# Two graph layers and routed experts on one core: further blocks in pairs, ring slots marked in fours

## What is computed

```python
h = relu(rgcn_conv(layernorm(x), W1, Wroot1, b1))     # both layers: the same edges
x = x + rgcn_conv(h, W2, Wroot2, b2)
x = x + experts(layernorm(x))                         # 2 of 8 experts for each node
# rgcn_conv:
xs = x[src]
seg = dst * R + etype
sums = segment_sum(xs, seg, N * R); cnt = segment_sum(ones, seg, N * R)
mean = (sums / maximum(cnt, 1)[:, None]).reshape(N, R, -1)
return x @ Wroot + b + einsum('nrd,rde->ne', mean, W)
```

## Time and profile before

| | us |
|---|---|
| median of three runs | 2933.71 |
| lowest, highest | 2932.59, 2935.83 |
| span of the profiled execution | 3487.9 |
| PE, VectorE, ScalarE busy in it | 2472.0, 1780.8, 1225.2 |
| GpSimd busy in it | 1862.5 |
| gathers L509 | 1584 of 964 ns |

### The profile page before, as it was taken

How to read it: one execution, slowest core, us unless ns; L and a number is a source line. 1 busy time by engine, 2 the same in 40 slices (tenths; PEclk the granted TensorE clock), 3 DMA queues, 4 the chain that set the end, 5 groups by cost and what they waited for, 6 DMA issues and landing times.

```text
span 3487.9 us, 82172 instructions
## 1 busy us (share of the span) xinstructions
PE 2472.0 (71%) x19212; PEld 1832.7 (53%) x19213; DVE 1780.8 (51%) x4984; ACT 1225.2 (35%) x2344; POOL 1862.5 (53%) x1980
## 2 busy tenths in 40 slices
PE   1346787678687786346776587687877428999999
PEld 0113565356365564114564365465656327888887
DVE  7324455345355454124454354354545338787777
ACT  5202343134243342012343143152432126555554
POOL 1666566655655554666556656655563543333333
PEclk9557999589799898557998798798997559999999
DMA  6223323233332232223333333333335234322222
GB/s 216 80 83 112 88 87 91 85 87 89 87 88 87 86 89 64 86 84 97 98 104 97 94 100 99 94 105 95 101 100 163 102 115 132 96 73 71 71 70 59
DMA packets 165489, 333.24 MB, mean 96 GB/s; under 512 B 36078, under 2 KB 102346, under 8 KB 165288
## 3 DMA queue, kind: packets, MB, share of 16 engines
q0 software_dynamic: 91632, 247.48, 24.1%
q1 hardware_dynamic: 39912, 41.03, 4.0%
q10 hardware_dynamic: 33872, 43.92, 3.9%
HBM read 285.39 MB, written 49.07 MB: 96 GB/s over the span
## 4 chain that ended last, share of the span: by engine, by line
PE 44%; issue 22%; DVE 10%; another core or an unknown queue 9%; DVEq 7%; SPq 2%; ACT 2%; DMA 1%; ACTq 0%; POOLq 0%; POOL 0%
PE more_banks L1408 13%; PE sum_banks L1384 9%; PE sum_banks L1385 7%; PE more_banks L1535 4%; PE sum_banks L1535 3%; PE more_banks L1400 3%; PE sum_banks L1545 3%; DVEq L1044 3%; DVEq L1041 2%; DVE sels L1044 2%; DVEq L1027 1%; DVE stage L1079 1%; DVE sels L1036 1%; PE sum_banks L1426 1%
## 5 line engine op out<-in xcount | busy, mean ns | idle before, releaser
L509 POOL DMA_INDIRECT ring<-table,tabs x1584 | 1526.9, 964 | 1046.4 <-SPq L399 670.0
L1384 PE MATMUL sum_banks<-ring,sels 128*128 x2348 | 726.6, 311 | 630.1 <-issue 420.1
L1408 PE MATMUL more_banks<-weights,stage 128*128 128x256 f16 x5292 | 919.1, 290 | 22.0 <-issue 21.4
L1385 PE MATMUL sum_banks<-ring,sels 128*128 x2348 | 732.2, 313 | 41.5 <-issue 38.7
L1384 PEld LDWEIGHTS sum_banks<-ring,sels 128*128 128x128 f16 (+1 forms) x2348 | 242.4, 103 | 928.2 <-issue 896.9
L683 ACT ACTIVATE stage<-sum_banks,inv 128x256 f16<-128x256 f32 x784 | 328.1, 473 | 789.5 <-issue 384.9
L1408 PEld LDWEIGHTS more_banks<-weights,stage 128*128 128x128 f16 x5292 | 531.1, 104 | 135.3 <-issue 37.1
L1036 DVE SCALAR_TENSOR_TENSOR sels<-lane,win_off,tabs 128x256 f16<-128x256 f16 x792 | 349.4, 482 | 422.1 <-remote 181.9
L654 ACT ACTIVATE stage<-more_banks 128x1024 f16<-128x1024 f16 x392 | 402.0, 1026 | 419.1 <-remote 405.6
L1044 DVE TENSOR_SCALAR sels<-lane,win_off,tabs 128x128 f16 x780 | 260.6, 334 | 495.8 <-issue 339.6
L1079 DVE SCALAR_TENSOR_TENSOR stage<-sum_banks,inv,stage 128x256 f16<-128x256 f32 x784 | 347.0, 479 | 57.2 <-issue 40.2
(11 more groups left out here) (319 smaller groups left out, 2407.5 us busy)
## 6 DMA issues: line engine op xcount, KB each, us to landing
ring<-table,tabs POOLq DMA_INDIRECT x1584
weights<-L_ffn_W ACTq DMA_DIRECT2D x96, 178.5 KB
stage<-L_ffn_W ACTq DMA_DIRECT2D x16, 1024.0 KB, 5.0
edge_work<-lot_in SPq DMA_DIRECT2D x54, 260.0 KB
table<-edge_work ACTq DMA_DIRECT2D x49, 128.0 KB
lot_in<-sels SPq DMA_DIRECT2D x8, 260.0 KB
weights<-L_gnn_W SPq DMA_DIRECT2D x2, 1024.0 KB, 8.3
weights<-L_gnn_W ACTq DMA_DIRECT2D x2, 1024.0 KB
```

What stands on the lines that cost most here:

```text
L509: pool.indirect_dma_start(ring_rows[:, b % RING, 0:2 * D], None, tables[layer], bass.IndirectOffsetOnAxis(row_tab[:, b:b + 1], 0)).then_in ...
L1384: pe.matmul(to[:, 0:D + 1], hot, ring_row[:, ds(at + D, D + 1)], start=first, stop=last, skip_group_check=True)
L1385: return pe.matmul(to[:, 0:D], hot, ring_row[:, ds(at, D)], start=False, stop=last, skip_group_check=True)
L1408: return [pe.matmul(ps_out[par], rows[:, xp * KD + k, :], w16[:, wp, k, r * D:(r + 1) * D], start=part == PART_ORDER[0] and n == 0, stop=p ...
```

## The change

Further blocks are taken two at a time. VectorE's loop makes two selections in one operation of 128 x 256, in the next of eight places of `sel_more`, and PE's loop adds two blocks and counts two steps at once. A window with an odd number of further blocks takes one block beyond its end; its selection is all zeros, since no edge of it belongs to the window. Both loops wait for the rows of both blocks. SyncE works in groups of four slots: it waits until four gathers have landed on one semaphore, or until all four slots are done with, and adds four. GpSimd waits for slots at every fourth gather. The setup computes the step counts for the padded numbers: two operations on rows of 392, and six on rows of 784 ahead of `turn_row`'s last use; `free_meta` has one number a group.

```diff
...
@@ -388,30 +396,30 @@
                 store_first(c)
 
             for layer in range(2):
-                regs = [sp.alloc_register(f"sp_free{layer}_{s}") for s in range(RING)]
-
-                def landed(turn, s):
-                    sp.wait_ge(gathered[s], turn * 16 + 16 * (USES[s] * layer + 1))
-                    sp.sem_inc(rows_ready[layer], 1)
-
-                def freed(s):
-                    sp.wait_ge(steps_done[layer], sp.snap(regs[s], donate=True) & MASK)
-                    sp.sem_inc(slots_free[layer], 1)
-                for s in range(AHEAD):
-                    landed(0, s)
+                regs = [sp.alloc_register(f"sp_free{layer}_{g}") for g in range(RING_GROUPS)]
+
+                def landed(turn, g):
+                    sp.wait_ge(gathered[g], turn * (16 * GROUP) + 16 * GROUP * (USES[g] * layer + 1))
+                    sp.sem_inc(rows_ready[layer], GROUP)
+
+                def freed(g):
+                    sp.wait_ge(steps_done[layer], sp.snap(regs[g], donate=True) & MASK)
+                    sp.sem_inc(slots_free[layer], GROUP)
+                for g in range(AHEAD):
+                    landed(0, g)
                 if layer == 0:
                     sp.wait_ge(tabs_set, 3 * COUNT + 3)
                 with sp.Fori(0, TURNS) as u:
-                    sp.load(regs, free_meta[0:1, ds(u * RING, RING)])
-                    for s in range(RING):
-                        freed(s)
-                        landed(u if s < AHEAD else u + 1, (s + AHEAD) % RING)
-                sp.load(regs, free_meta[0:1, TURNS * RING:(TURNS + 1) * RING])
-                for n in range(TURNS * RING, GATHERS - AHEAD):
-                    if n < TURNS * RING + OVER:
-                        freed(n % RING)
-                    landed((n + AHEAD) // RING, (n + AHEAD) % RING)
-                sp.sem_inc(rows_ready[layer], 1)
+                    sp.load(regs, free_meta[0:1, ds(u * RING_GROUPS, RING_GROUPS)])
+                    for g in range(RING_GROUPS):
+                        freed(g)
+                        landed(u if g < AHEAD else u + 1, (g + AHEAD) % RING_GROUPS)
+                sp.load(regs, free_meta[0:1, TURNS * RING_GROUPS:(TURNS + 1) * RING_GROUPS])
+                for n in range(TURNS * RING_GROUPS, GROUPS_ALL - AHEAD):
+                    if n < TURNS * RING_GROUPS + OVER:
+                        freed(n % RING_GROUPS)
+                    landed((n + AHEAD) // RING_GROUPS, (n + AHEAD) % RING_GROUPS)
+                sp.sem_inc(rows_ready[layer], GROUP)
                 for r in regs:
                     sp.free_register(r)
 
...
@@ -504,10 +512,10 @@
                 if layer == 1:
                     pool.wait_ge(table2_out, 16 * TILES)
                 for b in range(GATHERS):
-                    if b >= RING:
-                        pool.wait_ge(slots_free[layer], b - RING + 1)
+                    if b >= RING and b % GROUP == 0:
+                        pool.wait_ge(slots_free[layer], b - RING + GROUP)
                     pool.indirect_dma_start(ring_rows[:, b % RING, 0:2 * D], None, tables[layer],
-                                            bass.IndirectOffsetOnAxis(row_tab[:, b:b + 1], 0)).then_inc(gathered[b % RING], 16)
+                                            bass.IndirectOffsetOnAxis(row_tab[:, b:b + 1], 0)).then_inc(gathered[b % RING // GROUP], 16)
                 pool.drain()
 
             pool.wait_ge(sums_done[1], WPT * 14)
...
@@ -954,12 +962,15 @@
                 v.scalar_tensor_tensor(w_flat16[:, 1, :], w32, gnn_scale[:, layer:layer + 1], w_flat16[:, 0, :], ALU.mult, ALU.subtract).then_inc(w_split, 1)
             v.wait_ge(spans_ps, 2)
             lo, span, more, upto, one = (span_rows[0:1, k, :] for k in range(5))
+            padded = span_rows[0:1, 5, :].bitcast(i32)
             v.memset(one, 1.0)
             v.tensor_copy(lo, bank[4][0:1, 0:WINDOWS])
             link(v.tensor_copy(span, bank[5][0:1, 0:WINDOWS]))
             link(v.tensor_tensor(span, span, lo, ALU.subtract))
             link(v.tensor_scalar(more, span, -2.0, 0.0, ALU.add, ALU.max))
-            link(v.tensor_tensor_scan(upto, one, more, 0.0, ALU.mult, ALU.add))
+            link(v.tensor_scalar(padded, more, PAIR - 1.0, None, ALU.add))
+            link(v.tensor_scalar(padded, padded, (1 << 22) - PAIR, None, ALU.bitwise_and))
+            link(v.tensor_tensor_scan(upto, one, padded, 0.0, ALU.mult, ALU.add))
             v.memset(meta[0:1, WINDOWS:, 0], 2)
             v.memset(meta[0:1, WINDOWS:, 1], 0)
             for r in range(COUNT):
...
@@ -991,7 +1002,14 @@
             link(v.tensor_tensor(turn_row, last_row[:, 2:BLOCKS + 2], last_row[:, 1:BLOCKS + 1], ALU.subtract))
             link(v.scalar_tensor_tensor(left_row, left_row, 1.0, first_row, ALU.min, ALU.max))
             link(v.scalar_tensor_tensor(left_row, turn_row, 2.0, left_row, ALU.mult, ALU.add))
+            v.memset(kept_row[:, 0:1], 0.0)
             link(v.tensor_scalar(turn_row, turn_row, 1.0, None, ALU.min))
+            link(v.tensor_scalar(stay_row, turn_row, -1.0, 1.0, ALU.mult, ALU.add))
+            link(v.tensor_tensor_scan(kept_row[:, 1:BLOCKS + 1], stay_row, one_row, 0.0, ALU.mult, ALU.add))
+            link(v.scalar_tensor_tensor(first_row, kept_row[:, 0:BLOCKS], -1.0, first_row, ALU.mult, ALU.subtract))
+            link(v.tensor_scalar(pad_row, first_row, 2.0, 0.0, ALU.add, ALU.min))
+            link(v.tensor_scalar(pad_row, pad_row, PAIR - 1, None, ALU.bitwise_and))
+            link(v.tensor_tensor(left_row, left_row, pad_row, ALU.add))
             link(v.scalar_tensor_tensor(turn_row, left_row, -2.0, turn_row, ALU.add, ALU.mult))
             link(v.tensor_tensor_scan(free_src[:, 0:BLOCKS], one_row, turn_row, 0.0, ALU.add, ALU.add))
 
...
@@ -1036,13 +1054,18 @@
                 return v.scalar_tensor_tensor(sel[:, slot, h], lane16[:].unsqueeze(1).to_broadcast([P, 2, P]), win_off[:, ds(w, 1)],
                                               key_tab[:, ds((need - 2).with_bounds(min_val=0, max_val=GATHERS - 1), 2)].unsqueeze(2).to_broadcast([P, 2, P]), ALU.add, ALU.is_equal)
 
+            since = v.alloc_register("dve_since")
+
             def more_blocks(layer, need, end, w):
                 with v.If(end > need):
-                    with v.Fori(need & MASK, end) as i:
-                        v.wait_ge(rows_ready[layer], i + 1)
-                        block = i.with_bounds(min_val=0, max_val=GATHERS - 1)
-                        v.tensor_scalar(flat(sel_more[:, ds(block & (RING - 1), 1), :]), lane16[:], win_off[:, ds(w, 1)], key_tab[:, ds(block, 1)],
-                                        ALU.add, ALU.is_equal).then_inc(more_ready[layer], 1)
+                    with v.Fori(need & MASK, end, PAIR) as i:
+                        turn_no = v.snap(since, min_val=1, max_val=MASK)
+                        v.wait_ge(rows_ready[layer], i + PAIR)
+                        spot = ((turn_no & (SPOTS - 1)) * PAIR).with_bounds(min_val=0, max_val=RING - PAIR)
+                        v.scalar_tensor_tensor(sel_more[:, ds(spot, PAIR), :], lane16[:].unsqueeze(1).to_broadcast([P, PAIR, P]), win_off[:, ds(w, 1)],
+                                               key_tab[:, ds(i.with_bounds(min_val=0, max_val=GATHERS - 1), PAIR)].unsqueeze(2).to_broadcast([P, PAIR, P]),
+                                               ALU.add, ALU.is_equal).then_inc(more_ready[layer], 1)
+                        v.reg_add(since, since, 1)
 
             for layer in range(2):
                 def sums_out(t, par):
...
@@ -1388,11 +1413,15 @@
 
                 def more_sums(to, block, end):
                     with pe.If(end > block):
-                        with pe.Fori(block, end) as i:
+                        with pe.Fori(block, end, PAIR) as i:
+                            turn_no = pe.snap(since, min_val=1, max_val=MASK)
                             pe.wait_ge(more_ready[layer], since)
-                            slot = i & (RING - 1)
-                            at = (slot * PITCH).with_bounds(min_val=0, max_val=(RING - 1) * PITCH)
-                            add_rows(to, flat(sel_more[:, ds(slot, 1), :]), at, False, True).then_inc(steps_done[layer], 1)
+                            spot = (turn_no & (SPOTS - 1)) * PAIR
+                            for b in range(PAIR):
+                                hot = flat(sel_more[:, ds((spot + b).with_bounds(min_val=0, max_val=RING - 1), 1), :])
+                                at = ((i + b & (RING - 1)) * PITCH).with_bounds(min_val=0, max_val=(RING - 1) * PITCH)
+                                ins = add_rows(to, hot, at, False, True)
+                            ins.then_inc(steps_done[layer], PAIR)
                             pe.reg_add(since, since, 1)
 
                 def turn(c, slot):
```

(10 more changed lines are left out.)

30 lines of the change are left out of this document (18 added, 12 removed).

## The result

The changed kernel takes **3116.81 us** (median of four runs, 3116.47 to 3119.7) against 2933.72 us for the kernel before in the same comparison: ratio 1.0625, 95% interval 1.061 to 1.064. It is slower by 183 us. The prediction said 3065 us, slower, with a range of 2945 to 3150: the sign and the range held, the size of the loss was given as 131 us, which is 52 us too little.

The account below looks back on a forecast made before the run. Gathers (1.25 us each) bind heavy windows, the PE, VectorE and ScalarE path light ones. Layers 120 us, ends 5 and setup 6 make 131 us: 2933.7 + 131 = 3065 us, range 2945 to 3150.

Parts of the forecast that it names:

- The mechanism: PE's loop: register rows grow nearly as fast as turns fall, so windows with one further block cost 1.50 us against 0.70.
- The turn of two: PE's loop over further blocks: a turn of two blocks costs 1.74 us against 1.88 for two single turns.
- the added price: PE's turn: seven more rows of control, with two extra matmuls beside them, taken as 0.80 us.
- The signs named: Trace checks: 538 selections, 2644 matmuls a line, first matmul near 118 us, tile 12 at 24 to 26 us, longer slot waits.
- the scaling: Two layers: recorded durations scaled by 0.92 (+83 us) or 0.88 (+35) to fit 984 us; +60 a layer taken, 120 us.
- The sum by tiles: Each layer, the larger of gather pace and PE path per tile: 1068 us become 1158, +90 us a layer.
- Setup: VectorE's longer chain of operations before the first free slot: 6.3 us, exposed at GpSimd's wait, counted as 6 us.
- Ends of layers: Last gathers: blocks 788 to 790 wait for 791, some 2.5 us uncovered, twice: 5 us.
- Starvation by fours: GpSimd's queue of gathers running dry when slots are freed by fours: put at zero, kept as a rival.
- rival three: Gather queue starves by fours: up to 0.5 us a group, 100 us a layer; 3165 us with half; chance 0.11.
- Rival one: Layers: rows are hidden or gathers bind everywhere; 2960 us, or 2945 with no growth; chance 0.16.
- Rival two: Layers: faster, gathers well below 1.25 us and hand-over and branch the cost; 81 us a layer gained, 2783 us; chance 0.09.

Follow-up runs that it names:

- reuse: Changed kernel, but both blocks of PE's turn use the first block's selection and address: four matmuls, five register rows fewer; 3001.82 us (1.0233).
- half: Changed kernel, but PE's loop adds only the first block of each turn: 2 matmuls and 8 register rows; 3002.17 us (1.0241).
- second recording: The kernel before, unchanged, recorded once more: span 2936.2 us, 2938.31 us in its one run; the first recording's span was 3487.9 us.
- live5: Changed kernel with blocks and marks singly, plus nine register additions, packed into five rows, ahead of PE's loop per window with further blocks; 3248.81 us (1.1077).

## Why the prediction came out as it did

- **The mechanism held.** Register rows of PE's sequencer in the turn of a single further block are the largest part: 115 us by `reuse`, with the two matmuls free by `half`. The turn of two was put at 1.74 us and is 1.67; the added price was put at 0.80 and is 0.70 against before. The price of a row was right, 0.12 us; the count was seven, and it is six.
- **The signs named all came**: first matmul of the layers at 117.7 us (near 118 said), tile 12 at 24.8 us (24 to 26), tile 46 nearly unchanged, 538 selections, 2644 matmuls, waits for slots in tiles 13 to 27.
- **The step that failed is the scaling.** The sum by tiles gave +90 us a layer at recorded durations. Because its total (1068) did not fit the 984 us left by the runs, durations were scaled to 0.92 or 0.88 and +60 was taken. The layers grew by 101.6 and 62.4 us, 82 on average. In the second recording the durations that the sum took from layer 0 stand unscaled, and the misfit of 84 us has two other causes. First, 984 was 35 us too small. It rested on letting the last stage stand as it was in the first recording, 850 us from the last gather on and 31 between the layers; they are 791.9 and 23.1, and the layers have 1019 us on average from first to last gather. Second, the sum was too high, by 49 us against those 1019; counted from first matmul to last couple the layers took 1012 and 1009 us.
- **Where the sum was too high** differs by layer. In layer 0 it is the heavy tiles: 347.5 us said and 313 measured for tiles 0 to 5, 163.8 and 148 for 6 to 12, while 13 to 48 were nearly right (557 and 551). The form of the sum, the larger of gathers and path tile by tile, lets nothing pass from one tile to the next, but the ring can carry up to sixteen gathers (20 us) from a light tile into a heavy one: tile 1, with 47 blocks (58.8 us of gathers), took 47.0 us before. In layer 1 it is the light tiles: 557 us said and 512 measured for 13 to 48, since the sum took tile 46 of layer 0 for both layers, 13.65 us where layer 1 needs 12.05. Tiles 0 to 5 take 345 us there, as the sum has it, and tile 1 takes 57.1. That light tiles so near the gathers' pace leave the ring no lead would explain this, but no run tests it.
- **What the step cost.** Of the 52 us by which the prediction missed, 44 are the scaling (164 us measured in the layers, 120 taken). Unscaled, the sum gives 180 + 11 = 191 us against 183. That is in part luck: in tiles 13 to 48 the growth was put at 70.9 us and is 59, in tiles 0 to 5 of layer 0 it was put at nothing and is 20.
- **Setup, 6 us said, some 3 measured.** The chain is exposed at the seventeenth gather as said, but the layer's slack takes part of it back.
- **Ends of layers, 5 us said, 17.6 measured** (10.0 between the layers and 7.6 behind the second), and not for the reason given. With single blocks, marks by fours make neither end longer: GpSimd waits 21.7 us for the second layer's table instead of 25.5, and 789.1 us follow the last gather instead of 790.5. Pairs do, with single marks as well: 36.1 and 804.1 us. The last tile run, 9 to 12, has turns of its windows behind the last gather, and these grew; tile 12 alone grew by 5.6 us.
- **Starvation by fours, put at zero**, costs 22 to 31 us. That is a part of rival three, which had 100 to 200 us. Between the gathers of long loops the pace stays at 1.25 us; what the fours take lies mostly in tiles 0 to 5. That it is the ring's lead which they take back is argued, not shown.
- **Missing from the working**: that the row which computes the place from the turn number costs something even where blocks come singly. It is one of the rows of a pair's turn; alone it goes with 18 us.
- **Rival one** (rows hidden, or gathers bind everywhere) is out by `live5`. The Trainium skill's queue of 64 instructions (Advanced Engine Details and Errata, section Engine Queue Depths) doesn't hide the rows: `live5` lost 293 us by them. **Rival two** needed gathers faster than 0.94 us; they stayed at 1.25.

The account of the 183 us: setup 3, the place from the turn number about 20 with the selection's form, fours 22, padded turns and wider selection 24 (what is left, no run of its own), the second block's five register rows 115. They add to 184. Each is a difference of two medians from the runs above, in that order of building up; the kernel before itself moved by up to 4.5 us between the comparisons, so no term is surer than that.

## To carry to other kernels

In a loop with bounds in registers, count the register rows of a turn before its matmuls: here the rows set the pace and the matmuls were free. Taking blocks two at a time gained here only where windows were long; two thirds of the windows that had further blocks had exactly one, and paid 0.6 us each in tiles 13 to 48. Where two paces bound a pipeline by turns, sum over the stretches but let the ring between them carry its depth, and take the path from each layer for itself. When such a sum disagrees with the measured time, doubt the form of the sum and the recording before scaling the durations; a second recording settles it.

## What was not expected of the hardware

- A register row on PE costs some 0.12 us between weight loads (six for 0.70 us, five for 0.61), and 0.19 in the five packed rows of `live5` (0.97 us). One row more in 390 turns a layer went with 18 us of the whole.
- One recording of a kernel can be 19% longer than its runs (3487.9 us, and 2936.2 the second time) while the gathers (964 and 970 ns) and a light tile of layer 0 (13.65 and 13.58 us) in it agree with the undisturbed one.
- Two further matmuls of 256 columns in a turn of PE's loop cost nothing that can be measured (3001.82 and 3002.17 us with and without).
